# A macaron block in fp32: fc1, q and k of the middle batches as four column tiles of plain fp32 instead of three products of high and low parts

## The chip, the cores and the metric

One Trainium2 chip, one of its cores. The metric is the device time of the kernel in microseconds (us), the median over runs. The engines are named as the profile names them: PE (TensorE, matmuls), PEld (its weight loads), DVE (VectorE), ACT (ScalarE), POOL (GpSimd), SP (SyncE, which only issues DMAs here).

## The reference

The input x is [8, 512, 128]: 8 batches of 512 tokens with 128 features. A transformer block in macaron form is computed, all in fp32:

```
x = x + 0.5 * ffn(layernorm(x))            # the "pre" stage
x = x + attention(layernorm(x))            # x plus its output, normalised, times gamma, plus beta
x = x + 0.5 * ffn(layernorm(x))            # the "post" stage

ffn(x):  h = layernorm(x) * ln_gamma + ln_beta
         y = silu(h @ w1 + b1)             # fc1: 128 -> 512, w1 = (q - 128) * scale of the column
         return x + 0.5 * (y @ w2 + b2)    # fc2: 512 -> 128
attention(x): q, k, v = x @ w_qkv          # 16 heads of 8
         w = relu(q k^T / sqrt(8));  w = w / (sum(w) + 1e-6)
         y = x + (w v) @ w_out + b_out;  return layernorm(y) * gamma + beta
```

## The kernel before

**The grid of steps.** For each batch there are 16 steps: 4 groups of 4 heads times 4 tiles of 128 keys. In a step, `step_scores` (L659) makes the scores of four heads: four matmuls, each on 32 rows of the array (keys and queries as high and low parts in fp32r), 512 queries wide, into four banks of PSUM. ACT takes the relu of two banks (L981), DVE of the other two (L1280), into `probs`. `step_values(b, s - 1)` (L682) multiplies the probs of the step before with the values: four matmuls in plain fp32, each with 32 columns of weights, so that each has a column tile of the array of its own. A plain fp32 matmul stands in the records as two LDWEIGHTS and two MATMULs, so these four are "x8".

**What runs beside it.** All else is cut into small tasks that lists put beside the steps: `PE_ORDER[s]` has the tasks that PE does between the scores and the values of step s ("early") and after them ("late"), and `ACT_ORDER`, `DVE_ORDER` and `POOL_ORDER` say the same for their engines. The orders are written out by hand, each engine does its own strictly in this order, and semaphores tie them together. A name such as `pre.fc1.0@1` is the first quarter of fc1 of the pre stage, for the next batch; `post.fc1.0@-1` is that of the post stage, for the batch before. `*_START` are the lists for batch 0, `*_END` for batch 7, and `*_FIRST` and `*_LAST` stand ahead of and behind the grid: batch 0's pre stage and batch 7's post stage are done there in halves of the tokens (`edge`). "Middle batches" are pre stages of batches 1 to 7 and post stages of batches 0 to 6.

**An ffn in a middle batch.** `hT`: PE turns the normalised rows with four transposes (L596) into the stage's one PSUM bank; ACT copies them as fp32r, `t_hi` (L866); DVE subtracts that from the bank and gets `t_lo` (`low_t`, L1056), which frees the bank. `fc1.f` (f is 0 to 3, 128 of the 512 columns each) is three fp32r matmuls over the whole array, each 512 tokens wide: w_hi t_hi (L608), w_lo t_hi (L609), w_hi t_lo (L631). ACT takes the silu into `y` (L870). `fc2.f` is 16 small plain fp32 matmuls in column tiles (`by_tokens`, L603, x32).

**q and k in a middle batch.** `uT`: four transposes of `u1`; ACT copies twice, to `t_hi` (L878) and in full to `t_u` (L879); POOL subtracts the one from the other for `t_lo` (L1413). `k`, then `q`: the three products again, of which the third (L698) waits for POOL's low part. ACT and then DVE split the result in high and low parts (L887, L1103), and SP sends these to `k_op` and `q_op` by DMA; the scores of step 0 of the next batch wait for them. `v` works on `t_u` in column tiles (L603).

Within a batch the steps of PE that the change touches are: step 0 fc2.0 then pre fc1.0 (both late); step 1 fc2.1 to fc2.3 and pre fc1.1, then the values; step 2 pre fc1.2, then `post.op` (w_out), then the values; step 3 pre fc1.3, then the values; step 11, after the values, uT and post fc1.0; step 12, after the values, k and post fc1.1; step 13, after the values, q and post fc1.2; step 15 post fc1.3 and hT of the next batch, then the values. In batch 0 there is no post stage yet: fc1.0 to fc1.3 stand late in steps 1 to 4. The post fc1 of batch 6 stands in `PE_LAST`, behind the grid.

Of the kernel before, what the change touches and what calls it, by code (L numbers as in the profile page):

```python
# [11 lines left out]
P = 128  # L12
B, S, D = 8, 512, 128
H, HD = 16, 8
F = 512
# [104 lines left out]
    "weights.w1_hi", "first.hT.0", "first.hT.1", "first.fc1.0.1", "first.fc1.1.1",  # L120
    "first.fc1.2.1", "first.fc1.3.1", "first.uT.0", "first.t_u.0", "first.uT.1", "first.k0.0", "first.q0.0",
    "first.t_u.1", "first.q0.1", "first.v.0", "first.k0.1"
# [66 lines left out]
    ["first.k_lo.1"],  # L189
    ["pre.hT@1", "first.q_lo.1"],  # L190
    [],
# [11 lines left out]
    ["a.0"],  # L203
    ["pre.hT@2"],
]
# [10 lines left out]
    [],  # L216
    ["post.hT@-1"],
    [],
    ["oT.0", "den.0", "pre.k_lo@1"],
    ["pre.q_lo@1"],  # L220
    ["a.0"],
    ["pre.hT@2"],
]
# [15 lines left out]
    ["den.0"],  # L239
    ["a.0", "post.hT@-1"],  # L240
]
# [10 lines left out]
POOL_START = [  # L252
    "post.u_bias", "v_in.2", "pre.x_stats@2", "v_in.3", "pre.x1_stats@1", "pre.u_apply@1", "pre.uT@1", "pre.x_apply@2",
    "v_in.0@1", "v_in.1@1", "pre.x1_beta@1", "pre.xr@2"
# [8 lines left out]
    ["pre.u_apply@1"],  # L263
    ["pre.x_stats@2", "pre.uT@1"],
    [],
# [43 lines left out]
def build(nc, x, w_qk, w_v, w_out, fc1_q, fc2_q, fc2_scales, columns, lines, out):  # L309
# [4 lines left out]
    with ExitStack() as ctx:  # L314
        def sb(name, shape, dtype=F32):
            return ctx.enter_context(nc.sbuf_tensor(name, shape, dtype))
# [11 lines left out]
        s2_rows = sb("s2_rows", [P, FT, D])  # L328
        w1_hi, w1_lo = sb("w1_hi", [P, F], F32R), sb("w1_lo", [P, F], F32R)

        wqk = sb("wqk", [P, 4, D])
# [13 lines left out]
        class Stage:  # L345


            def __init__(self, n, fills, buffers):
                self.fills = fills
                self.two_x = [sb(f"{n}_x{i}", [P, TT, D]) for i in range(buffers)]  # L350
                self.h = sb(f"{n}_h", [P, TT, D])
                self.xr = sb(f"{n}_xr", [P, TT, D])
                self.t_hi, self.t_lo = sb(f"{n}_t_hi", [P, S], F32R), sb(f"{n}_t_lo", [P, S], F32R)
                self.y = sb(f"{n}_y", [P, FT, S])
                self.bank = psum(f"{n}_bank", [P, S])
                self.full, self.free = sem(f"{n}_bank_full"), sem(f"{n}_bank_free")
                self.mixed = sem(f"{n}_mixed")
                self.t_hi_in = sem(f"{n}_t_hi_in")
                self.full_a, self.free_a = sem(f"{n}_full_first_half"), sem(f"{n}_free_first_half")
                self.t_hi_a = sem(f"{n}_t_hi_first_half")  # L360
                self.rows, self.rows_by_t, self.res = sem(f"{n}_rows"), sem(f"{n}_rows_by_t"), sem(f"{n}_residual")
# [137 lines left out]
        b1_added, b1_link, b1_ready, b2_ready = sem("b1_added"), sem("b1_link"), sem("b1_ready"), sem("b2_ready")  # L499
        w_link, w2_link, wqk_link = sem("w_link"), sem("w2_link"), sem("wqk_link")  # L500
        w1_ready, w2_ready, wqkv_ready = sem("w1_ready"), sem("w2_ready"), sem("wqkv_ready")
        ident_ready, ident_zero, warm_ready, v_ready = sem("ident_ready"), sem("ident_zero"), sem("warm_ready"), sem("v_ready")
# [76 lines left out]
        def _(pe):  # L579
# [19 lines left out]
            def by_tokens(into, tokens, t, w, start, stop):  # L599
# [4 lines left out]
                return last  # L604

            def two_products(into, w_hi, w_lo, t_hi):

                mm(into, w_hi, t_hi, start=True, stop=False)  # L608
                mm(into, w_lo, t_hi, start=False, stop=False)  # L609

            def ffn(st, b, what):
                if what == "hT":
                    if st is pre and b == 1:

                        pe.wait_ge(*emptied(pre, 0, "v"))
                    else:
                        next_fill(st, b, "hT")
                    if st is post:
                        pe.wait_ge(y_done, b + 1)
                    transposes(st, b, st.h, st.rows)  # L620
                elif what.startswith("fc1"):
                    f = int(what[-1])
                    cols, into = slice(P * f, P * (f + 1)), fc1_bank(st, b, f)
                    if st is post and b == B - 2:

                        pe.wait_ge(probs_done[f // 2][f % 2], STEPS * B)
                        pe.wait_ge(post.free, len(POST_FILLS) * b + post.n("hT"))
                    else:
                        next_fill(st, b, what)
                    two_products(into, w1_hi[:, cols], w1_lo[:, cols], st.t_hi[:, :])  # L630
                    mm(into, w1_hi[:, cols], st.t_lo[:, :], start=False, stop=True).then_inc(st.full, 1)  # L631
                elif what.startswith("fc2"):
                    f = int(what[-1])
                    if f == 0 and not (st is post and b == B - 2):
                        next_fill(st, b, "fc2")
                    pe.wait_ge(st.free, len(st.fills) * b + st.n(f"fc1.{f}"))
                    for t in range(TT):
                        last = by_tokens(st.bank, st.y[:, f, :], t, w2[:, f, :], f == 0 and t == 0, f == FT - 1 and t == TT - 1)
                    if f == FT - 1:
                        last.then_inc(st.full, 1)  # L640
# [45 lines left out]
            def task(stage, what, b):  # L686
                if stage == "pre":
# [4 lines left out]
                    elif what in ("q", "k"):  # L692
                        i = "qk".index(what)
                        next_fill(pre, b, what)
                        pe.wait_ge(u_hi_in, b + 1)
                        two_products(pre.bank[:, :], wqk_hi[:, i, :], wqk_lo[:, i, :], pre.t_hi[:, :])
                        pe.wait_ge(u_lo_in, b + 1)
                        mm(pre.bank[:, :], wqk_hi[:, i, :], pre.t_lo[:, :], start=False, stop=True).then_inc(pre.full, 1)  # L698
                    elif what == "v":
# [21 lines left out]
            def edge(st, b, what, h):  # L721
# [17 lines left out]
                elif what.startswith("fc1"):  # L739
                    f = int(what[-1])  # L740
                    weights, to = slice(P * f, P * (f + 1)), scores[f // 2][:, f % 2, cols]
                    pe.wait_ge(*of_half(st.t_hi_a, st.t_hi_in, h, b))
                    if st is pre:
# [108 lines left out]
        def _(act):  # L852
# [5 lines left out]
            def ffn(st, b, what):  # L858
                per = len(st.fills)
                if what == "hT":  # L860
                    act.wait_ge(st.full, per * b + st.n("hT"))
                    if st is pre and b == 1:

                        act.wait_ge(q_made, 1)

                    activation(st.t_hi[:, :], st.bank[:, :], ACT.Copy).then_inc(st.t_hi_in, 1)  # L866
                elif what.startswith("fc1"):
# [5 lines left out]
            def task(stage, what, b):  # L873
                if stage == "pre":
                    per = len(PRE_FILLS)
                    if what == "uT":
                        act.wait_ge(pre.full, per * b + pre.n("uT"))
                        activation(pre.t_hi[:, :], pre.bank[:, :], ACT.Copy).then_inc(u_hi_in, 1)  # L878
                        activation(t_u[:, :], pre.bank[:, :], ACT.Copy).then_inc(pre.free, 1)  # L879
# [74 lines left out]
            def prepare_w1_hi():  # L954
# [3 lines left out]
                activation(w1_hi[:, :], w1[:, :], ACT.Copy, scale=g_col).then_inc(w_link, 1)  # L958

            def work(b, names):  # L960
                for stage, what, tb in tasks(b, names):
                    if stage == "weights":
                        prepare_w1_hi()
                    elif stage in ("first", "last"):
                        edge(pre if stage == "first" else post, tb, what[:-2], int(what[-1]))
                    else:
                        task(stage, what, tb)
# [19 lines left out]
        def _(dve):  # L987
# [65 lines left out]

            def low_t(st, hi_in, count, done):
                dve.wait_ge(hi_in, count)
                v.tensor_tensor(st.t_lo[:, :], st.bank[:, :], st.t_hi[:, :].bitcast(F32), ALU.subtract  # L1056
                                ).then_inc(done, 1)

            def task(stage, what, b):
# [22 lines left out]
                elif stage == "pre":  # L1082
                    per = len(PRE_FILLS)
                    if what == "x_stats":
                        dve.wait_ge(x_loaded[b % 2], 16 * (b // 2 + 1))
                        row_stats(norm_x, b, pre.x(b))
                    elif what == "hT":
                        low_t(pre, pre.t_hi_in, b + 1, pre.free)
                    elif what == "x1":
# [16 lines left out]
                elif stage == "post":  # L1106
# [18 lines left out]
                    elif what == "x2_stats":  # L1125
                        dve.wait_ge(x2_done, b + 1)
                        row_stats(norm_x2, b, post.x(b))
                    elif what == "hT":
                        low_t(post, post.t_hi_in, b + 1, post.free)
                    elif what == "out":  # L1130
# [34 lines left out]
            def edge(st, b, what, h):  # L1165
# [27 lines left out]
                elif what == "hT":  # L1193
                    dve.wait_ge(*of_half(st.t_hi_a, st.t_hi_in, h, b))
                    v.tensor_tensor(st.t_lo[:, cols], turn_bank(st, h)[:, cols], st.t_hi[:, cols].bitcast(F32), ALU.subtract
# [90 lines left out]
        def _(pool):  # L1286
# [103 lines left out]
            def task(stage, what, b):  # L1390
# [11 lines left out]
                elif stage == "pre":  # L1402
# [6 lines left out]
                    elif what == "xr":  # L1409
                        residual(norm_x, pre, b)  # L1410
                    elif what == "uT":
                        pool.wait_ge(pre.free, len(PRE_FILLS) * b + pre.n("uT"))
                        p.tensor_tensor(pre.t_lo[:, :], t_u[:, :], pre.t_hi[:, :].bitcast(F32), ALU.subtract  # L1413
                                        ).then_inc(u_lo_in, 1)
                    elif what == "x1_stats":
# [100 lines left out]
```

## Time and profile before

| | us |
|---|---|
| median of 3 runs | 370.05 (369.62 to 370.37) |
| span of the profiled execution (first to last instruction) | 369.5 |
| from the values of step 1 of one middle batch (152.05) to those of the next | 43.0 |
| PE busy | 360.0 (97%) |
| DVE busy | 283.8 (77%) |
| ACT busy | 231.4 (63%) |
| POOL busy | 219.8 (59%) |
| granted TensorE clock | 1.000 of full |

"Busy" of PE is the union of its matmuls' spans from start to modelled end. Matmuls are pipelined, and the next one starts before the last one's end; so what a group of matmuls costs is read from its start to the start of the next group, and a short wait between two groups does not show as idle time. The chain that ended last is 87% PE, 4% DVE and 2% each of ACT, DMA, POOL and issue.

### The profile page before, as it was taken

The page shows a single profiled execution, that of the slowest core. Times are in us where ns is not written, and L with a number is a line of the kernel's source. Part 1 is how long each engine was busy: PE and PEld are TensorE (multiplying, and loading weights), DVE is VectorE, ACT ScalarE, POOL GpSimd, SP SyncE. Part 2 cuts the span into 40 slices and gives each one's busy share as a digit, 9 for nine tenths or more (in the row PEclk, how much of TensorE's full clock was granted, in tenths as well). Part 3 has the DMA queues.
Part 4 walks back from the last instruction along what each step waited for, and adds up shares of the span by engine and source line. Part 5 has one row for each costly group of instructions (what it writes and reads, how often), then busy time and mean ns, then how long its engine had stood idle before and what let it go on. Part 6 is the DMA issues. An engine that isn't in the chain of part 4 may idle for free.

```text
span 369.5 us, 11752 instructions
## 1 busy us (share of the span) xinstructions
PE 360.0 (97%) x4518; PEld 185.2 (50%) x4518; DVE 283.8 (77%) x689; ACT 231.4 (63%) x425; POOL 219.8 (59%) x447
## 2 busy tenths in 40 slices
PE   8999998999999999999999999999999999999996
PEld 8854433453564445653564434644456535532476
DVE  5876677897778977699777977689776797578774
ACT  3377465667847586466865678475864668588523
POOL 7595065547973589437992479635894377315541
PEclk9999999999999999999999999999999999999999
DMA  7016005500351005500173003610063001710001
GB/s 211 4 31 173 3 0 128 131 3 2 88 143 60 3 0 136 147 8 1 31 173 87 4 0 67 165 59 2 4 156 104 4 0 32 191 38 2 2 2 61
DMA packets 14103, 22.66 MB, mean 61 GB/s; under 512 B 2528, under 2 KB 3808, under 8 KB 14048
## 3 DMA queue, kind: packets, MB, share of 16 engines
q1 hardware_dynamic: 11456, 17.83, 20.1%
q10 hardware_dynamic: 2592, 4.07, 3.4%
q8 instruction: 37, 0.61, 0.7%
q14 instruction: 18, 0.15, 0.1%
HBM read 3.54 MB, written 2.10 MB: 15 GB/s over the span
## 4 chain that ended last, share of the span: by engine, by line
PE 87%; DVE 4%; ACT 2%; DMA 2%; issue 2%; POOL 2%; SPq 0%; POOLq 0%; DVEq 0%; ACTq 0%
PE o_bank L682 30%; PE scores L659 16%; PE pre_bank L603 9%; PE post_bank L603 9%; PE pre_bank L608 5%; PE pre_bank L609 3%; DMA q_op<-q_parts 2%; PE pre_bank L631 2%; PE post_bank L608 2%; PE pre_bank L596 1%; PE post_bank L609 1%; PE post_bank L631 1%; PE o_bank L590 1%; PE post_bank L596 1%; PE scores L608 1%
## 5 line engine op out<-in xcount | busy, mean ns | idle before, releaser
L1280 DVE TENSOR_SCALAR probs<-scores 128x512 f32<-128x512 f32 x242 | 155.8, 683 | 48.3 <-PE scores L659 45.0
L981 ACT ACTIVATE probs<-scores 128x512 f32<-128x512 f32 x262 | 141.7, 596 | 65.9 <-PE scores L659 65.9
L682 PE MATMUL o_bank<-probs,v_op 128*32 128x512 f32 x1024 | 135.9, 602 | 0.2
L659 PE MATMUL scores<-q_op,k_op 32*128 32x512 f32 x504 | 76.0, 494 | 1.9 <-DMA q_op<-q_parts 0.8
L659 PEld LDWEIGHTS scores<-q_op,k_op 32*128 32x128 f32 x504 | 31.9, 181 | 81.5 <-issue 54.4
L870 ACT ACTIVATE pre_y<-pre_bank,b_sum,col_consts 128x512 f32<-128x512 f32 x28 | 21.9, 782 | 23.6 <-PE pre_bank L631 23.5
L682 PEld LDWEIGHTS o_bank<-probs,v_op 128*32 128x32 f32 x1024 | 21.9, 108 | 28.4 <-issue 24.6
L603 PE MATMUL pre_bank<-w,pre_y 128*32 128x128 f32 x960 | 30.8, 274 | 0.0
L603 PEld LDWEIGHTS pre_bank<-w,pre_y 128*32 128x32 f32 x960 | 25.7, 110 | 8.1 <-issue 7.7
L603 PE MATMUL post_bank<-w,post_y 128*32 128x128 f32 x960 | 29.3, 273 | 0.0
L603 PEld LDWEIGHTS post_bank<-w,post_y 128*32 128x32 f32 x960 | 25.9, 110 | 5.6 <-issue 5.4
L1309 POOL TENSOR_SCALAR norm_x_var<-norm_x_mv 128x4 f32<-128x4 f32 x21 | 4.1, 197 | 39.5 <-DVE norm_x_mv L1051 39.0
L1309 POOL TENSOR_SCALAR norm_y_var<-norm_y_mv 128x4 f32<-128x4 f32 x7 | 1.4, 200 | 43.6 <-DVE norm_y_mv L1051 43.6
L1312 POOL TENSOR_TENSOR norm_x_rs<-norm_x_var,minus_half 128x4 f32<-128x4 f32 x21 | 21.2, 1009 | 1.8
L870 ACT ACTIVATE post_y<-post_bank,b_sum,col_consts 128x512 f32<-128x512 f32 x24 | 18.7, 780 | 0.7
L1447 POOL TENSOR_TENSOR y_rows<-y_rows,rows 128x512 f32<-128x512 f32 x7 | 9.0, 1292 | 16.5 <-ACT y_rows L906 14.3
L1382 POOL TENSOR_TENSOR v_op<-v_rows,v_op 128x128 f32<-128x128 f32 (+1 forms) x33 | 13.6, 420 | 6.4 <-ACT v_rows L892 6.4
L1349 POOL TENSOR_TENSOR norm_x_rs<-norm_x_var,minus_half 128x4 f32<-128x4 f32 x16 | 16.2, 1015 | 1.3
L1365 POOL TENSOR_SCALAR pre_xr<-pre_x,norm_x_mix 128x128 f32<-128x128 f32 x32 | 15.6, 501 | 0.8
L608 PE MATMUL pre_bank<-pre_t_hi,w_hi 128*128 128x512 f32 x28 | 14.0, 499 | 0.9 <-DVE pre_t_lo L1056 0.5
L1340 POOL TENSOR_SCALAR u<-x,norm_x_rs,norm_x_shift 128x128 f32<-128x128 f32 x28 | 12.3, 455 | 1.5 <-POOL norm_x_shift L1316 1.5
L1340 POOL TENSOR_SCALAR post_h<-post_x,norm_x_rs,norm_x_shift 128x128 f32<-128x128 f32 x28 | 12.3, 455 | 1.2 <-POOL norm_x_shift L1316 1.1
(219 smaller groups left out, 555.3 us busy)
## 6 DMA issues: line engine op xcount, KB each, us to landing
k_op<-k_parts SPq DMA_DIRECT2D x62, 128.0 KB, 2.7
q_op<-q_parts SPq DMA_DIRECT2D x62, 128.0 KB, 2.7
out_dram<-o_rows ACTq DMA_DIRECT2D x7, 256.0 KB, 2.0
pre_x<-in_x_dram ACTq DMA_DIRECT2D x6, 256.0 KB, 2.8
w_int<-in_L_ffn_fc_q_dram SPq DMA_DIRECT2D x2, 256.0 KB, 3.9
rows<-in_lines_dram ACTq DMA_DIRECT2D x1, 256.0 KB, 6.0
s_rows<-in_L_ffn_fc_scales_dram SPq DMA_DIRECT2D x1, 256.0 KB, 6.6
wqk<-in_w_qk_dram SPq DMA_DIRECT2D x1, 256.0 KB, 6.7
```

What stands on the lines that cost most here:

```text
L603: last = mm(into[VW * j:VW * (j + 1), P * t:P * (t + 1)], tokens[:, part], w, start=start, stop=stop)
L608: mm(into, w_hi, t_hi, start=True, stop=False)
L609: mm(into, w_lo, t_hi, start=False, stop=False)
L659: mm(score_bank(b, s, i, j), k_op[rows, g, P * kt:P * (kt + 1)], q_op[rows, g, :], start=True, stop=True).then_inc(scores_done[i], 1)
L682: last = mm(o_bank[pair][VW * j:VW * (j + 1), :], v_op[:, kt, heads_of(g).start + 2 * j, :], probs[:, s % 2, j, :], start=(odd == 0 and kt ...
L870: activation(st.y[:, f, :], fc1_bank(st, b, f), ACT.Silu, bias=b1_sum[:, f:f + 1], scale=s1_col[:, f:f + 1]).then_inc(st.free, 1)
L981: activation(probs[:, s % 2, 2 * i + j, :], score_bank(b, s, i, j), ACT.Relu).then_inc(probs_done[i][j], 1)
L1280: v.tensor_scalar(probs[:, s % 2, 2 * i + j, :], score_bank(b, s, i, j), 0.0, None, ALU.max).then_inc(probs_done[i][j], 1)
L1312: p.tensor_tensor(norm.rs[:, i, :], norm.var[:, i, :], minus_half[:, i, :], ALU.pow).then_inc(norm.rs_in, 1)
L1340: last = p.tensor_scalar(dst[:, t, :], rows[:, t, :], norm.rs[:, i, t:t + 1], norm.shift[:, i, t:t + 1], ALU.mult, ALU.add)
L1349: p.tensor_tensor(norm.rs[:, 0, :], norm.var[:, 0, :], minus_half[:, 0, :], ALU.pow).then_inc(norm.half_in, 1)
L1365: last = p.tensor_scalar(st.xr[:, t, :], st.x(b)[:, t, :], norm.mix[:, 0, t:t + 1], norm.mix[:, 1, t:t + 1], ALU.mult, ALU.add)
```

## The change

In middle batches (`ffn` and `task` on PE, not `edge`) the three products are replaced by `by_columns`: four plain fp32 matmuls, each with 32 of the 128 weight columns, each on all 512 tokens, into 32 partitions of the bank. The tokens are one full fp32 copy: `st.t` (new) for fc1, and `t_u`, which is there already, for q and k. The weights are `w1_whole` (new, g times w1 in full, made once by ACT ahead of the grid) and `wqk`.

```diff
+            def by_columns(into, w, tokens):
+                for j in range(HG):
+                    part = slice(VW * j, VW * (j + 1))
+                    last = mm(into[part, :], w[:, part], tokens, start=True, stop=True)
+                return last
...
-                    two_products(into, w1_hi[:, cols], w1_lo[:, cols], st.t_hi[:, :])
-                    mm(into, w1_hi[:, cols], st.t_lo[:, :], start=False, stop=True).then_inc(st.full, 1)
+                    if f == 0 and st is pre and b == 1:
+                        pe.wait_ge(w1_whole_in, 1)
+                    by_columns(into, w1_whole[:, cols], st.t[:, :]).then_inc(st.full, 1)
...
-                        pe.wait_ge(u_hi_in, b + 1)
-                        two_products(pre.bank[:, :], wqk_hi[:, i, :], wqk_lo[:, i, :], pre.t_hi[:, :])
-                        pe.wait_ge(u_lo_in, b + 1)
-                        mm(pre.bank[:, :], wqk_hi[:, i, :], pre.t_lo[:, :], start=False, stop=True).then_inc(pre.full, 1)
+                        by_columns(pre.bank[:, :], wqk[:, i, :], t_u[:, :]).then_inc(pre.full, 1)
...
                     if st is pre and b == 1:
                         act.wait_ge(q_made, 1)
-                    activation(st.t_hi[:, :], st.bank[:, :], ACT.Copy).then_inc(st.t_hi_in, 1)
+                        act.wait_ge(*emptied(pre, 1, "k"))
+                    activation(st.t[:, :], st.bank[:, :], ACT.Copy).then_inc(st.free, 1)
...
-                        activation(pre.t_hi[:, :], pre.bank[:, :], ACT.Copy).then_inc(u_hi_in, 1)
                         activation(t_u[:, :], pre.bank[:, :], ACT.Copy).then_inc(pre.free, 1)
...
+            def prepare_w1_whole():
+                activation(w1_whole[:, :], w1[:, :], ACT.Copy, scale=g_col).then_inc(w1_whole_in, 1)
```

The low parts go with it: `low_t` on DVE (`pre.hT`, `post.hT` out of `DVE_START`, `DVE_ORDER` and `DVE_END`) and the subtraction on POOL (`pre.uT` out of `POOL_START` and `POOL_ORDER`). `weights.w1_whole` comes into `ACT_FIRST`, behind the last silu of the first pre stage. No task changes its place in the lists of PE.

## Rows read from the trace of the kernel before

**Rows 1.** The page's busy times: busy us (share of the span) x instructions.

```profile
PE 360.0 (97%) x4518; PEld 185.2 (50%) x4518; DVE 283.8 (77%) x689; ACT 231.4 (63%) x425; POOL 219.8 (59%) x447
```

**Rows 2.** Timeline of PE, step 5: start us, us, engine line op out<-in xcount.

```profile
161.50 1.06 PE L682 MATMUL o_bank<-probs,v_op 128*32 128x512 f32 x8
162.38 1.06 PE L603 MATMUL pre_bank<-w,pre_y 128*32 128x128 f32 x32
163.37 0.51 PE L659 MATMUL scores<-q_op,k_op 32*128 32x512 f32 x4
```

**Rows 3.** Timeline of PE, steps 11 and 12 of the same batch.

```profile
175.37 0.65 PE L596 MATMUL pre_bank<-ident,u 128*128 128x128 f32 x4
175.78 0.48 PE L608 MATMUL post_bank<-post_t_hi,w_hi 128*128 128x512 f32 x1
...
176.66 0.51 PE L659 MATMUL scores<-q_op,k_op 32*128 32x512 f32 x4
177.10 1.07 PE L682 MATMUL o_bank<-probs,v_op 128*32 128x512 f32 x8
178.09 0.50 PE L608 MATMUL pre_bank<-pre_t_hi,wqk_hi 128*128 128x512 f32 x1
...
178.90 0.39 PE L608 MATMUL post_bank<-post_t_hi,w_hi 128*128 128x512 f32 x1
...
179.69 0.51 PE L659 MATMUL scores<-q_op,k_op 32*128 32x512 f32 x4
```

**Rows 4.** Timeline of PE, step 15 of the same batch.

```profile
185.46 0.50 PE L608 MATMUL post_bank<-post_t_hi,w_hi 128*128 128x512 f32 x1
...
186.26 0.60 PE L596 MATMUL pre_bank<-ident,pre_h 128*128 128x128 f32 x4
186.79 1.07 PE L682 MATMUL o_bank<-probs,v_op 128*32 128x512 f32 x8
```

**Rows 5.** Timeline of PE, steps 1 and 2 of the same batch.

```profile
148.40 2.83 PE L603 MATMUL post_bank<-w,post_y 128*32 128x128 f32 x96
151.16 0.50 PE L608 MATMUL pre_bank<-pre_t_hi,w_hi 128*128 128x512 f32 x1
...
152.05 1.06 PE L682 MATMUL o_bank<-probs,v_op 128*32 128x512 f32 x8
153.05 0.50 PE L659 MATMUL scores<-q_op,k_op 32*128 32x512 f32 x4
...
154.38 1.08 PE L603 MATMUL post_bank<-wo,aT 128*32 128x128 f32 x32
155.28 1.04 PE L682 MATMUL o_bank<-probs,v_op 128*32 128x512 f32 x8
```

**Rows 6.** Busy in two stretches: stretch, us, busy (x) per engine, PEclk, DMA share, GB/s.

```profile
155.28:173.75 18.47, 18.47 (x247) 8.07 (x239) 16.75 (x51) 11.37 (x23) 8.75 (x20) 1.00 0.10 31
163.20:172.25 9.05, 9.05 (x131) 4.10 (x119) 8.72 (x26) 4.52 (x9) 4.65 (x11) 1.00 0.01 2
```

**Rows 7.** Timeline of DVE, steps 10 to 12, with idle time before and its releaser.

```profile
173.81 0.68 DVE L1056 TENSOR_TENSOR post_t_lo<-post_bank,post_t_hi 128x512 fp32r<-128x512 f32 x1
...
177.30 1.29 DVE L1280 TENSOR_SCALAR probs<-scores 128x512 f32<-128x512 f32 x2 [1.61 <-PE scores L659]
```

**Rows 8.** What PE waited for, the whole span: us in total, times, longest.

```profile
PE scores L659 <- DMA q_op<-q_parts: 0.8, 1, 0.8
...
PE pre_bank L608 <- DVE pre_t_lo L1056: 0.5, 1, 0.5
```

**Rows 9.** Timeline of PE, k in step 12 of batch 0.

```profile
51.91 0.50 PE L608 MATMUL pre_bank<-pre_t_hi,wqk_hi 128*128 128x512 f32 x1
...
53.09 0.49 PE L698 MATMUL pre_bank<-pre_t_lo,wqk_hi 128*128 128x512 f32 x1 [0.45 <-POOL pre_t_lo L1413]
```

**Rows 10.** Timeline of PE behind the grid: the bias, then three quarters of fc1, then w_out.

```profile
349.00 0.70 PE L807 MATMUL pre_bank<-u_bias,ident 128*128 128x256 f32 x2
...
351.81 0.65 PE L603 MATMUL pre_bank<-wo,aT 128*32 128x128 f32 x16
```

More of the change, by code:

```diff
@@ L120 @@
     "weights.w1_hi", "first.hT.0", "first.hT.1", "first.fc1.0.1", "first.fc1.1.1",
-    "first.fc1.2.1", "first.fc1.3.1", "first.uT.0", "first.t_u.0", "first.uT.1", "first.k0.0", "first.q0.0",
+    "first.fc1.2.1", "first.fc1.3.1", "weights.w1_whole", "first.uT.0", "first.t_u.0", "first.uT.1", "first.k0.0", "first.q0.0",
     "first.t_u.1", "first.q0.1", "first.v.0", "first.k0.1"
@@ L189 @@
     ["first.k_lo.1"],
-    ["pre.hT@1", "first.q_lo.1"],
+    ["first.q_lo.1"],
     [],
@@ L203 @@
     ["a.0"],
-    ["pre.hT@2"],
+    [],
 ]
@@ L216 @@
     [],
-    ["post.hT@-1"],
+    [],
     [],
@@ L221 @@
     ["a.0"],
-    ["pre.hT@2"],
+    [],
 ]
@@ L239 @@
     ["den.0"],
-    ["a.0", "post.hT@-1"],
+    ["a.0"],
 ]
@@ L252 @@
 POOL_START = [
-    "post.u_bias", "v_in.2", "pre.x_stats@2", "v_in.3", "pre.x1_stats@1", "pre.u_apply@1", "pre.uT@1", "pre.x_apply@2",
+    "post.u_bias", "v_in.2", "pre.x_stats@2", "v_in.3", "pre.x1_stats@1", "pre.u_apply@1", "pre.x_apply@2",
     "v_in.0@1", "v_in.1@1", "pre.x1_beta@1", "pre.xr@2"
@@ L263 @@
     ["pre.u_apply@1"],
-    ["pre.x_stats@2", "pre.uT@1"],
+    ["pre.x_stats@2"],
     [],
@@ L329, in build @@
         w1_hi, w1_lo = sb("w1_hi", [P, F], F32R), sb("w1_lo", [P, F], F32R)
+        w1_whole = sb("w1_whole", [P, F])
         wqk = sb("wqk", [P, 4, D])
@@ L352, in __init__ @@
                 self.xr = sb(f"{n}_xr", [P, TT, D])
+                self.t = sb(f"{n}_t", [P, S])
                 self.t_hi, self.t_lo = sb(f"{n}_t_hi", [P, S], F32R), sb(f"{n}_t_lo", [P, S], F32R)
@@ L500, in build @@
         w_link, w2_link, wqk_link = sem("w_link"), sem("w2_link"), sem("wqk_link")
+        w1_whole_in = sem("w1_whole_in")
         w1_ready, w2_ready, wqkv_ready = sem("w1_ready"), sem("w2_ready"), sem("wqkv_ready")
@@ L741, in edge @@
                     weights, to = slice(P * f, P * (f + 1)), scores[f // 2][:, f % 2, cols]
-                    pe.wait_ge(*of_half(st.t_hi_a, st.t_hi_in, h, b))
+                    pe.wait_ge(st.t_hi_in if h else st.t_hi_a, 1)
                     if st is pre:
@@ L962, in work @@
                     if stage == "weights":
-                        prepare_w1_hi()
+                        (prepare_w1_whole if what == "w1_whole" else prepare_w1_hi)()
                     elif stage in ("first", "last"):
@@ L1052, in row_stats @@
                 last.then_inc(norm.measured, 1)
[L1054 to L1057, printed above, removed]
             def task(stage, what, b):
@@ L1086, in task @@
                         row_stats(norm_x, b, pre.x(b))
-                    elif what == "hT":
-                        low_t(pre, pre.t_hi_in, b + 1, pre.free)
                     elif what == "x1":
@@ L1127, in task @@
                         row_stats(norm_x2, b, post.x(b))
-                    elif what == "hT":
-                        low_t(post, post.t_hi_in, b + 1, post.free)
                     elif what == "out":
@@ L1193, in edge @@
                 elif what == "hT":
-                    dve.wait_ge(*of_half(st.t_hi_a, st.t_hi_in, h, b))
+                    dve.wait_ge(st.t_hi_in if h else st.t_hi_a, 1)
                     v.tensor_tensor(st.t_lo[:, cols], turn_bank(st, h)[:, cols], st.t_hi[:, cols].bitcast(F32), ALU.subtract
@@ L1410, in task @@
                         residual(norm_x, pre, b)
[L1411 to L1414, printed above, removed]
                     elif what == "x1_stats":
```

## The prediction

> **What bounds the kernel now.** I read the page's busy times first: PE 97%, DVE 77%, the others about 60% [rows 1]. That alone would call PE the bound everywhere. Since matmuls are pipelined, I then went through PE's timeline for one middle batch and took each group from its own start to the next group's start ("slot"), since short waits hide in those. A batch repeats every 43.0 us (the table above has it). Its 16 steps fall in two kinds of stretch.
>
> From the values of step 2 (155.28) to the scores of step 11 (173.75) there are 18.47 us, of which DVE is busy 16.75; in the 9.05 us from 163.20 it is busy 8.72, without a gap worth the name [rows 6]. This is a chain from w_out over y, its statistics, POOL's and ACT's normalisation, x2, x1, the statistics and the relus. PE's groups there have slots stretched by waits. In this stretch the only edited group is pre fc1.3.
>
> From step 11 on, and through steps 0, 1 and 2 of the next batch, DVE waits for PE (1.61 us idle before the relu of step 12 [rows 7]) and PE's slots stand back to back. Nine of a batch's ten edited groups are there. So the change is worth what it does to PE's slots in steps 11 to 2, and nearly nothing in steps 3 to 10.
>
> **The slots on both sides.** Two things set a slot: the stream itself, and a switch between kinds of tiling. A group of plain fp32 column tiles of 512 tokens is in the trace already, the values matmul, with the same shapes as the new groups. Followed by another group in column tiles it takes 162.38 - 161.50 = 0.88 us [rows 2]. Followed by matmuls over the whole array it takes 178.09 - 177.10 = 0.99 [rows 3], by scores in row tiles 1.00 [rows 5]. A fc2 group followed by scores takes 0.99 [rows 2]. So a change of tiling costs 0.10 to 0.12, and a new group costs 0.88 inside a run of column groups and 0.98 at its end. Three products cost 0.81 (k) and 0.79 (fc1.1) where they stand behind each other [rows 3], 0.80 with transposes behind them [rows 4], 0.88 before scores [rows 3] and 0.89 before the values [rows 5].
>
> The unknown is whether four tiles that all stream the same 512 tokens go like four that stream different ones. Bounds: 0.86 (a bit under the 0.88, if the shared stream saves reads) and 1.07 (the full length of a values group, nothing overlapped [rows 3]). I take 0.88: the values have the shape, and fc2, whose four tiles do stream one and the same w2, 128 wide, goes through as many columns in the same 0.88 (0.99 with its switch [rows 2]).
>
> **The change part by part.**
> Step 11: before, uT 0.41 and fc1.0 0.88, 1.29 in all [rows 3]. After, the transposes have to switch into column tiles as well: 0.53 with a like group before them [rows 4], plus about 0.06 for the entry, 0.59; then 0.98. +0.28.
> Step 12: before, values 0.99, k 0.81, fc1.1 0.79, 2.59 [rows 3]. After, one run of column tiles: 0.88 + 0.88 + 0.97 = 2.73, or 2.71 as a values group behind another column group takes a trifle less. +0.13. Step 13 (q and fc1.2) has the same pattern: +0.13.
> Step 15: before, fc1.3 0.80 and hT 0.53 [rows 4]. After, 0.98 and 0.59. +0.24.
> Steps 11 to 15 together: +0.78.
> Step 0: fc2.0 no longer switches (-0.11), fc1.0 ends at scores, 0.98 for 0.89: -0.03.
> Step 1: before, three fc2 groups 2.76, fc1.1 0.89, values 1.00, 4.65 [rows 5]. After, 2.65 + 0.88 + 0.97 = 4.50: -0.15.
> Step 2: fc1.2, then w_out, 0.90 [rows 5]: both become 0.88, -0.04. Steps 0 to 2 together: -0.22.
> Step 3: fc1.3, behind it the DVE chain; 0.
>
> Steps 11 to 13 change in batches 1 to 6 (6 x 0.54 = 3.24); step 15 in batches 1 to 5 with a hT behind it (5 x 0.24 = 1.20), in batch 6 without one (-0.04). Steps 0 to 2 change in full in batches 2 to 6 (5 x -0.22 = -1.10); in batch 1 there is no post stage to run with, about -0.13. Middle: +3.17 us.
>
> The removed work. DVE's low part (0.68 [rows 7]) goes twice a batch, 1.4 us of DVE; ACT's second copy and POOL's subtraction go once. I price them at nothing in the middle batches, since they stand where DVE has time: the one in step 10 comes after the relu that PE waits for, the one in step 15 has idle time around it. Bounds: 0 and, if all of DVE's relief reached the chain, -1.4 per batch. I take 0 as DVE idles 1.61 us right behind the first [rows 7].
>
> POOL's tasks behind the removed one (v_in.3, the next x_apply, xr) move about 1.3 us ahead, past nothing that waits. The wait added on ACT (hT of batch 1 behind the DVE's k_lo) queues the copy, then first.q and fc1.0's silu; the old order had the low part behind the same k_lo on DVE, so the bank was not free earlier either. 0, or at most once the 0.68 of such a pass [rows 7]. `w1_whole` on ACT is one pass of 128x512 behind the last silu of the first fc1 and ahead of uT, which must wait for fc2, x1, its statistics and POOL: these hide it, 0; uncovered it would be about as long as DVE's pass, 0.7, once. No DMA is moved, but those of q_op follow q: by the slots above q ends later against step 11, and the run from q to step 0 grows by 0.4, so the DMA has more room, not less.
>
> Start. In batch 0 PE waits 0.5 us for DVE's low part ahead of fc1.0 [rows 8]: gone, and the values before it no longer switch (-0.12), while fc1.0 takes 0.98 for 0.90: -0.53. Then in step 12 the low product of k starts 1.18 us behind the high one, as POOL is late [rows 9]; the group, about 1.55 with some 0.37 for its last slot, becomes 0.98, and starts 0.11 sooner: -0.7. What follows is the chain k, q, DMA, for which the scores of batch 1 wait 0.8 [rows 8]; about -0.6 of it gets through, the rest to the DVE. Three more fc1 of batch 0 at -0.01 each. Start: -1.15.
>
> End. From the bias (349.00) to w_out (351.81) there are 2.81 us with nine products [rows 10]. One is 0.23 (fc1.1's 0.79 less a switch of 0.10, over three [rows 3]); without them 0.71 is left. With three column groups 0.71 + 2.64 = 3.35, or 3.20 if the bias takes less of it: +0.45, all on the chain, since w_out opens the last DVE chain. The post hT of batch 6 is off it.
>
> Sum: +3.17 - 1.15 + 0.45 = +2.5 us. The profiled span is 369.5; after, 372.0. The median of the runs is 370.05, 0.55 above that span, so I forecast 372.5.
>
> A rule against the row. At steady stream a product over the whole array is 0.23 us, three of them 0.70, and four fp32 column tiles are 0.88: the column form is slower as arithmetic, by 0.18, and only the switches that it saves pay that back. The Trainium skill ("FP8 and Floating Point Precision", TensorE Precision Notes) states that true FP32 takes four passes through the array, one for each pairing of high and low halves, where the old code does three of the four. By that rule alone the group would cost 4 x 0.23 = 0.93, and all 70 groups would add 16 us. The trace has 0.88, slightly better than the rule, and its switches take most of the difference away.
>
> **The rivals.**
> A, the likeliest: as above, 372.5. Chance 0.55.
> B, faster: DVE's relief gets through. If the 1.4 us a batch that DVE saves shortened the stretch in which it sets the pace, six batches would give back 8.4: 370.05 + 2.5 - 8.4 = 364.2. For: DVE is busy 16.75 of 18.47 there [rows 6]. Against: the removed work does not lie in that stretch but right behind it (173.81 [rows 7]) and in step 15. A part of it (0.5 a batch) would give 369.5. Chance 0.14.
> C, no change: the entry into the transposes costs nothing (0.53 stays) and column groups take 0.86. That is -0.12 per batch and -0.02 on 60 groups, 2 us less, 370.5. For: the slots are read to 0.01 to 0.03. Chance 0.15.
> D, slower by more: four tiles on one token stream get in each other's way (1.07 per group, the upper bound). On the 58 groups outside the DVE stretch, 0.1 to 0.19 each: 378 to 383. For: no row has one stream of 512 in four tiles. Against: fc2 has one of 128 in four tiles and loses nothing [rows 2]. Chance 0.1.
> E, the rule of four passes without the switches: each group outside the DVE stretch +0.18 to +0.23, 381 to 385. The Trainium skill's page named above speaks for it. Against: steps 12 and 1, where the switches are in the rows. Chance 0.06.
>
> **How the numbers follow.** What a measurement of this kernel tells from no change is about 0.2%, 0.7 us. Case A spreads by some 1.5 us, 371 to 374; its lower edge and C fill the interval around the old time; B lies below. Faster 0.15, same 0.15, slower 0.70. The range 369.6 to 375.5 takes A whole, C, and the partial form of B, and leaves out the full B, most of D, and E.
>
> **What would show it.** In the timeline after, the values, k and fc1.1 of step 12 start 0.88 apart with the scores 0.97 behind; the transposes of steps 11 and 15 take 0.59; steps 3 to 10 keep their 18.5 us; fc1.0 of batch 0 starts without a wait and scores of batch 1 about 1.1 us earlier than before; the batch period goes from 43.0 to 43.55. It would be wrong if a column group with a shared stream takes over 0.95 in a run, if the stretch of steps 3 to 10 gets shorter than 18 us, or if scores of a step 0 wait for the DMA.

## The result

| | before | after |
|---|---|---|
| median, us | 370.21 (369.62 to 370.37, 4 runs) | 372.67 (372.30 to 372.85, 4 runs) |
| ratio to before | 1 | 1.0063, 95% interval 1.0049 to 1.0078 |
| span of the profiled execution | 369.5 | 370.9 |
| PE / DVE / ACT / POOL busy | 360.0 / 283.8 / 231.4 / 219.8 | 363.0 / 275.2 / 229.4 / 208.6 |

The changed kernel is slower by 2.5 us, 0.6%. The median before is 0.16 above the one in the table of the old kernel, since a fourth run has come in. DVE, ACT and POOL all have less to do, PE has more.

The page's busy times after (busy us, share of the span, instructions), against [rows 1]:

```profile
PE 363.0 (98%) x4868; PEld 166.9 (45%) x4868; DVE 275.2 (74%) x675; ACT 229.4 (62%) x419; POOL 208.6 (56%) x440
```

The timeline of PE after, steps 11 and 12 of a middle batch, which answers to [rows 3]. The new groups are line L613.

```profile
174.29 0.66 PE L599 MATMUL pre_bank<-ident,u 128*128 128x128 f32 x4
174.87 1.07 PE L613 MATMUL post_bank<-post_t,w_whole 128*32 128x512 f32 x8
175.87 0.51 PE L670 MATMUL scores<-q_op,k_op 32*128 32x512 f32 x4
176.31 1.06 PE L693 MATMUL o_bank<-probs,v_op 128*32 128x512 f32 x8
177.19 1.04 PE L613 MATMUL pre_bank<-t_u,wqk 128*32 128x512 f32 x8
178.05 1.04 PE L613 MATMUL post_bank<-post_t,w_whole 128*32 128x512 f32 x8
179.02 0.51 PE L670 MATMUL scores<-q_op,k_op 32*128 32x512 f32 x4
```

From start to start: uT 0.58 (0.41 before), fc1.0 1.00 (0.88); in step 12 values 0.88 (0.99), k 0.86 (0.81), fc1.1 0.97 (0.79). The whole of step 12 is 3.15 instead of 3.03.

The same for step 15, against [rows 4]:

```profile
184.91 1.06 PE L613 MATMUL post_bank<-post_t,w_whole 128*32 128x512 f32 x8
185.91 0.66 PE L599 MATMUL pre_bank<-ident,pre_h 128*128 128x128 f32 x4
186.50 1.07 PE L693 MATMUL o_bank<-probs,v_op 128*32 128x512 f32 x8
```

fc1.3 is 1.00 and hT 0.59, where 0.80 and 0.53 stood. And steps 1 and 2, against [rows 5]:

```profile
147.52 2.83 PE L606 MATMUL post_bank<-w,post_y 128*32 128x128 f32 x96
150.17 1.04 PE L613 MATMUL pre_bank<-pre_t,w_whole 128*32 128x512 f32 x8
151.03 1.04 PE L693 MATMUL o_bank<-probs,v_op 128*32 128x512 f32 x8
152.00 0.51 PE L670 MATMUL scores<-q_op,k_op 32*128 32x512 f32 x4
152.43 1.07 PE L613 MATMUL pre_bank<-pre_t,w_whole 128*32 128x512 f32 x8
153.32 1.06 PE L606 MATMUL post_bank<-wo,aT 128*32 128x128 f32 x32
```

Here the neighbours are column groups. From start to start the three fc2 groups, fc1.1 and the values take 2.65, 0.86 and 0.97, for 2.76, 0.89 and 1.00 before: a run of column groups pays one change of tiling, at its end.

The stretch from the values of step 2 to the scores of step 11, against the first of [rows 6] (columns as there):

```profile
154.19:172.67 18.48, 18.48 (x253) 7.85 (x245) 16.78 (x51) 11.44 (x23) 8.76 (x20) 1.00 0.10 30
```

It lasts 18.48 us as before (18.47), with DVE busy 16.78 (16.75). DVE's idle time before the relu of step 12 has grown from 1.61 [rows 7] to 1.91, with the low part gone ahead of it:

```profile
173.31 1.29 DVE L1283 TENSOR_SCALAR probs<-scores 128x512 f32<-128x512 f32 x2 [0.49 <-PE scores L670]
176.51 1.29 DVE L1283 TENSOR_SCALAR probs<-scores 128x512 f32<-128x512 f32 x2 [1.91 <-PE scores L670]
```

### The profile page after: what moved, and what is told of

Its sections match the earlier page's. It is cut to its first block, busy times and chain, and to the rows that moved or that the text cites. A ratio compares the mean times of both kernels' runs of the same rounds, so it can differ in the third digit from the quotient of the medians.

```text
span 370.9 us, 12412 instructions
## 1 busy us (share of the span) xinstructions
PE 363.0 (98%) x4868; PEld 166.9 (45%) x4868; DVE 275.2 (74%) x675; ACT 229.4 (62%) x419; POOL 208.6 (56%) x440
## 4 chain that ended last, share of the span: by engine, by line
PE 88%; DVE 5%; DMA 2%; ACT 2%; issue 1%; SPq 0%; POOL 0%; DVEq 0%; ACTq 0%
PE o_bank L693 31%; PE scores L670 17%; PE pre_bank L613 10%; PE pre_bank L606 9%; PE post_bank L606 8%; PE post_bank L613 6%; PE pre_bank L599 2%; DMA s_rows<-in_L_ffn_fc_scales_dram 2%; PE post_bank L599 1%; DVE probs L1283 1%; PE scores L613 1%; PE scores L618 1%; DVE norm_x_stats L1054 0%; ACT probs L993 0%; ACT y_rows L914 0%
## 5 line engine op out<-in xcount | busy, mean ns | idle before, releaser
L693 PEld LDWEIGHTS o_bank<-probs,v_op 128*32 128x32 f32 x1024 | 23.3, 108 | 31.5 <-issue 30.2
L613 PE MATMUL pre_bank<-pre_t,w_whole 128*32 128x512 f32 x224 | 29.5, 598 | 0.5 <-ACT pre_y L879 0.5
L613 PE MATMUL post_bank<-post_t,w_whole 128*32 128x512 f32 x192 | 25.3, 598 | 0.0
L613 PE MATMUL pre_bank<-t_u,wqk 128*32 128x512 f32 x112 | 14.6, 594 | 0.1
```

The source lines that it names most:

```text
L613: last = mm(into[part, :], w[:, part], tokens, start=True, stop=True)
L693: last = mm(o_bank[pair][VW * j:VW * (j + 1), :], v_op[:, kt, heads_of(g).start + 2 * j, :], probs[:, s % 2, j, :], start=(odd == 0 and kt ...
```

## The experiments

All are compared with the kernel before on the same chip; intervals are 95%. "Column tiles" are `by_columns`, as in the change.

**The kernel before once more.** No edit.

> The kernel of before itself, timed against itself, to see how far two identical programs fall apart and how much of a run's time lies outside its span. Ratio 1.000, within 0.2%. The profiled execution of before has a span of 369.5 and the changed kernel's 370.9, which is 1.4 apart, while their medians are 2.5 apart. Theory 1: the time around the span differs between the two profiled executions by chance, and before's is about 0.7 to 1 here again or anywhere up to 2. Theory 2: the changed kernel has more around its span than before has in all its runs.

Measured: 369.90, ratio 0.9998 (0.9987 to 1.0008), span 367.9 for an execution of 369.75. So the time around the span is 1.85, about as for the changed kernel (372.85 and 370.9, 1.95), and the first trace, with 369.5, was a long execution of the old kernel: over 27 executions of before in this comparison the spans go from 367.6 to 369.1. Of the 1.6 us that it had more, 0.7 lie ahead of the grid (the first scores of batch 0 start at 21.47, for 20.77 in the second trace), 0.7 where batch 1 begins, and 0.2 where batch 5 begins. In the first trace PE waits 0.8 for the DMA of q_op where batch 1 begins [rows 8]; in the second, PE's timeline shows no idle time before these scores (L659):

```profile
59.32 1.07 PE L682 MATMUL o_bank<-probs,v_op 128*32 128x512 f32 x8
60.46 0.50 PE L659 MATMUL scores<-q_op,k_op 32*128 32x512 f32 x4
```

The slot of these values is 1.14, though, for 1.00 elsewhere, and 0.99 at this place in the changed kernel: a wait of some 0.15 hides in it, so the DMA wait was smaller in this execution and not wholly absent. Of the two theories the first holds, if with 1.85 and not the 0.7 to 1 thought likelier: the two medians, not the two first spans, tell the change. The comparisons of places below use this second trace.

**Only pre fc1 in column tiles.** The edit in short, not in the kernel's words:

```diff
-    by_columns(into, w1_whole[:, cols], st.t[:, :])            # all middle fc1, q, k
+    by_columns(...) if st is pre else three products           # q, k: three products
```

> Only fc1 of the pre stage (steps 0 to 3, where its neighbours are column tiles) is in column tiles; post fc1, q and k stay three products. Theory of the switches: steps 0 to 2 give back 0.22 in five batches and 0.13 in batch 1, batch 0 gives 0.7 (no wait for DVE's low part), -1.9 in all: 368.3. Rival, a column group costs 0.18 more than three products wherever it stands (0.88 against 0.70): 28 groups, +5.0: 375.2. Rival, the gain of the whole change at the start is all from k and q: 369.0.

Measured: 367.70, ratio 0.9935 (0.9921 to 0.9950). The first 16 steps take 38.83 us (39.69 before), a middle batch 42.76 (43.00). The theory of the switches gave 368.3, which is within the interval; the price by the group (375.2) and the gain all from k and q (369.0) are not. This half of the change is a gain.

**Only post fc1, q and k in column tiles.** The complement of the last one.

> The other half alone: post fc1, q and k in column tiles (steps 11 to 15 and behind the grid), pre fc1 stays three products. Theory of the switches: +0.54 in steps 11 to 13 of six batches, +0.24 in step 15 of five, +0.45 at the end, -1.4 in batch 0 for k and q, +3.5 in all: 373.7. With only-pre-fc1 it should add up to the whole change. Rival, 0.18 a group wherever it stands: 42 groups, +7.6, less 1.4: 376.4.

Measured: 374.94, ratio 1.0130 (1.0113 to 1.0148), 1.2 above the 373.7 expected. Batches 3 to 5 take 43.79 to 43.81, 0.80 more than before, which is the working of the prediction (0.78). The excess lies elsewhere: batch 0 gives 0.76 back and not 1.4, since most of the DMA wait of the first trace is not there in the second; batch 6 takes 0.2 and batch 7 takes 0.28 more than expected (both below); and batch 2 takes 44.15, as a relu on DVE starts some 0.36 late in its step 8 (at 124.83, 1.00 behind the scores), for which the trace names no releaser but these scores. The rival's 376.4 is outside the interval. The two halves add up: -2.5 and +4.7 make +2.2 where the whole change has +2.5.

**DVE's low parts put back, unused.** The edit in short:

```diff
-    activation(st.t[:, :], st.bank[:, :], ACT.Copy).then_inc(st.free, 1)
+    activation(st.t[:, :], st.bank[:, :], ACT.Copy).then_inc(st.t_hi_in, 1)
+    # DVE, at its old places:
+    v.tensor_tensor(st.t_lo, st.bank, st.t, ALU.subtract).then_inc(st.free, 1)
```

> The changed kernel with DVE's two subtractions per batch put back where they were (they free the bank again, and nobody reads what they write). Theory: worth nothing in the middle batches, about 0.5 to 0.6 in batch 0 where fc1.0 waits for DVE: 372.7 + 0.6 = 373.3. Rival, DVE's relief is part of what keeps the change at only +0.7%: DVE is over 90% busy in steps 3 to 10, 0.5 to 1.4 per batch come back: 376 to 381.

Measured: 372.99, ratio 1.0078 (1.0063 to 1.0094), not to be told from the 1.0063 (1.0049 to 1.0078) without them. A middle batch takes 43.55 to 43.57, as without them (43.53 to 43.56). Only batch 0 has them: 38.94 for 38.25, and PE's timeline shows the wait of [rows 8] back again ahead of fc1.0:

```profile
25.94 1.07 PE L632 MATMUL pre_bank<-pre_t,w_whole 128*32 128x512 f32 x8 [0.49 <-DVE pre_t_lo L1103]
```

So 9.6 us of DVE work (14 passes of 0.69) are worth nothing but this one wait, and the rival's 376 to 381 is out.

**ACT's second copy and POOL's subtraction put back, and k waits for it.** The edit in short:

```diff
+    activation(pre.t_hi[:, :], pre.bank[:, :], ACT.Copy).then_inc(u_hi_in, 1)    # ACT, uT
+    p.tensor_tensor(pre.t_lo, t_u, pre.t_hi, ALU.subtract).then_inc(u_lo_in, 1)  # POOL
+    pe.wait_ge(u_lo_in, b + 1)                                                   # PE, before k and q
```

> The changed kernel with ACT's second copy of uT and POOL's subtraction put back, and k waiting for the subtraction although it doesn't read it. Theory: in batch 0 k is late again as before, +0.6 to 0.8; in the middle batches the subtraction ends about 3.1 us after uT starts, and k, which now follows the values 0.11 sooner and has no high products to do first, would wait some 0.2 to 0.3 in each of six batches: 372.7 + 2.2 = 374.9. Rival, the wait is as free in the middle batches as it was before the change: 373.4.

Measured: 376.91, ratio 1.0180 (1.0164 to 1.0195), 2 us above what I expected. Batches 2 to 5 take 43.96 to 44.01, 0.44 more than the changed kernel and not 0.2 to 0.3. The timeline of a middle batch in steps 11 and 12 has the reason:

```profile
176.34 0.66 PE L618 MATMUL pre_bank<-ident,u 128*128 128x128 f32 x4
...
178.19 1.28 POOL L1466 TENSOR_TENSOR pre_t_lo<-t_u,pre_t_hi 128x512 fp32r<-128x512 f32 x1 [0.42 <-ACT t_u L925]
...
179.62 1.07 PE L632 MATMUL pre_bank<-t_u,wqk 128*32 128x512 f32 x8 [0.20 <-POOL pre_t_lo L1466]
```

The subtraction ends 3.13 after uT's start, as I had reckoned (3.1). But k starts 0.15 behind that end, 3.28 after uT, where the changed kernel has it at 2.90 (177.19 - 174.29): 0.38 later. PE's idle time before k, 0.20, shows only half of this, since it counts from the modelled end of the values; step 12 as a whole goes from 3.15 to 3.56. Batch 0 takes 1.38 more, for 0.6 to 0.8 expected. What PE waited for in the whole execution has a second item that I had not thought of:

```profile
PE pre_bank L632 <- POOL pre_t_lo L1466: 2.4, 7, 1.2
...
PE scores L695 <- DMA q_op<-q_parts: 1.1, 1, 1.1
```

The 2.4 are 1.2 in batch 0 and 0.2 in each of six batches. The 1.1 stand once, before batch 7. Of q's two transfers there one took 2.6 us to land and the other 4.5, for 2.5 and 2.6 in the changed kernel. The slow one was issued at 317.7 and so was in at 322.2, and the scores start at 322.25; with 2.6 it would have been in at 320.3, before they were due (321.2). So it was the slow landing and not the later q alone; why it was slow is not shown. The rival, a wait free in the middle batches, is out: the three products had hidden POOL behind their two high products; a single group that needs all of t at its start has nothing to hide it with. That the change takes t_u whole is thus not a side issue.

**Two tasks exchanged in the changed kernel.**

```diff
-    ([], ["pre.uT@1", "post.fc1.0@-1"]),       # PE_ORDER, step 11
+    ([], ["post.fc1.0@-1", "pre.uT@1"]),
-    (["post.fc1.3@-1", "pre.hT@2"], []),       # PE_ORDER, step 15
+    (["post.fc1.3@-1"], ["pre.hT@2"]),
-    ["pre.hT@2", "post.fc1.3@-1"],             # ACT_ORDER, step 15
+    ["post.fc1.3@-1", "pre.hT@2"],
```

> The changed kernel with two tasks of PE exchanged so that a change of tiling falls away: in step 11 post fc1.0 goes ahead of uT, directly behind the values; in step 15 the values go ahead of hT (and ACT takes fc1.3's silu first). No instruction is added or removed. Theory, a change of tiling costs 0.10 to 0.14: -0.13 in six batches and -0.14 in five: 372.7 - 1.5 = 371.2. Rival, the column groups are dear by themselves and the order doesn't matter: 372.7. Other rival, uT or hT is late for k or for fc1.0 then: over 373.

Measured: 371.21, ratio 1.0028 (1.0019 to 1.0037). With the same instructions in another order 1.5 us are gone by the medians and 1.3 by the trace, from the first scores to w_out behind the grid. In steps 11 and 15 each of the 11 places is shorter by 0.12 to 0.16, as worked out from one change of tiling less; batch 6 gives 0.12 of it back in step 13 (below). Both rivals, 372.7 and over 373, are out. PE's timeline of the new step 11:

```profile
172.45 1.06 PE L718 MATMUL o_bank<-probs,v_op 128*32 128x512 f32 x8
173.33 1.04 PE L632 MATMUL post_bank<-post_t,w_whole 128*32 128x512 f32 x8
174.30 0.66 PE L618 MATMUL pre_bank<-ident,u 128*128 128x128 f32 x4
174.89 0.51 PE L695 MATMUL scores<-q_op,k_op 32*128 32x512 f32 x4
```

0.88, 0.97, 0.59: 2.44 us where the changed kernel has 1.00, 0.58, 1.00, 2.58. A middle batch takes 43.28 instead of 43.55.

One rival to the word "tiling" remains. The column groups are also the plain fp32 ones, so where such a group ends both the tiling and the form of the products change. The kernel before has a place where only the tiling changes, from fp32r over the whole array to fp32r in row tiles, in PE's timeline of step 0:

```profile
147.41 0.40 PE L609 MATMUL pre_bank<-pre_t_hi,w_lo 128*128 128x512 f32 x1
147.64 0.39 PE L631 MATMUL pre_bank<-pre_t_lo,w_hi 128*128 128x512 f32 x1
147.96 0.51 PE L659 MATMUL scores<-q_op,k_op 32*128 32x512 f32 x4
```

The third product takes 0.32 to the next start, the second 0.23. So a change of tiling alone costs 0.09 there. That it makes up all of the 0.10 to 0.14 behind a column group was not tried.

**Column tiles only where they pay.** pre fc1 of all batches, and q and k of batch 1.

```diff
+def fc1_by_columns(stage, b):
+    return stage == "pre"
+def qk_by_columns(b):
+    return b == 1
```

> Column tiles where their neighbours are column tiles or where the low part was late: pre fc1 in all batches, q and k of batch 1 (done during batch 0); post fc1 and the other q and k stay three products. Theory: only-pre-fc1 measured 367.7; q and k of batch 1 give back another 0.6, as the first 16 steps took 38.25 with them and 38.83 without: 367.1, 0.8% under the kernel before. Rival, the two gains of batch 0 overlap: 367.7.

Measured: 367.01, ratio 0.9918 (0.9903 to 0.9932), 3 us under the kernel before and, by the two ratios, 5.4 under the changed one. The first 16 steps take 38.24, as in the changed kernel, a middle batch 42.75. These first steps speak against the rival, by which the two gains overlap (367.7); the median alone hardly would, as its interval ends at 367.5. PE's timeline has k of batch 1 directly behind the values, and the scores (L695) 0.98 later, where [rows 9] have a wait of 0.45 inside k:

```profile
49.53 1.06 PE L718 MATMUL o_bank<-probs,v_op 128*32 128x512 f32 x8
50.41 1.04 PE L632 MATMUL pre_bank<-t_u,wqk 128*32 128x512 f32 x8
51.39 0.51 PE L695 MATMUL scores<-q_op,k_op 32*128 32x512 f32 x4
```

## Why the prediction was right, step by step

Forecast 372.5, measured 372.67. The terms, from the starts of the scores of step 0 of each batch in PE's timeline (second trace of before against the changed kernel):

| | predicted | measured |
|---|---|---|
| batch 0 | -1.15 | 39.69 to 38.25: -1.44 |
| batch 1 | +0.65 | 39.88 to 40.72: +0.84 |
| batches 2 to 5 | +0.56 each | 43.00 to 43.02, then 43.53 to 43.56: +2.17 in all |
| batch 6 | +0.28 | 42.57 to 43.04: +0.47 |
| batch 7 up to its last scores | 0 | 29.33 to 29.61: +0.28 |
| from there to w_out | +0.45 | 5.88 to 6.29: +0.41 |

These sum to +2.73. What is left of the two spans is +0.6 ahead of the grid and -0.4 in the last store. The first is larger or smaller from one execution to the next: the first scores start at 20.77 and 21.47 in the two traces of the old kernel, at 20.72 to 21.40 in the others. The second is not: from the start of DVE's last addition to the end of the span the old kernel takes 2.84 and 2.93, all seven kernels with an edit 2.55 to 2.63. So some 0.3 us are gained there that nobody had priced, and with them the sum comes to +2.4, as the medians have it (+2.46). The cause was not looked for.

*Luck in the total.* The forecast lies within 0.2 us of the measured time, which is closer than its terms are. Batch 0 gave 0.3 more than predicted and the last store another 0.3, while batches 1 and 6 took 0.2 each and batch 7 0.3 more. The forecast span of 372.0 was 1.1 above the measured one (370.9), since it was worked out from the span of a long execution; the 0.55 that was then added for the time around the span was as much too small (1.95 measured), and the two errors cancel. And two figures of the rivals do not fit: the partial form of B, 369.5, lies just outside the range that was said to take it in, and 58 groups at 0.18 to 0.23 give 380.5 to 383.4 for E and not 381 to 385.

*The slots.* Right in each place: 0.85 to 0.89 inside a run of column groups, 0.97 to 1.00 at its end, 0.58 to 0.59 for the transposes that now enter from column tiles. That four tiles with one stream of 512 tokens go like four with different ones was the unknown, and is now in the rows after. Rival D (the shared stream) is out by these rows, and so is the entry without a cost of rival C (0.59 for 0.53), though its 0.86 for a group between column groups came true; that the order of tasks alone moves 1.5 us shows that the switch has a price of its own beside the group's. Rival E, a group dearer by 0.18 wherever it stands, is out by the first half alone, faster by 0.65% with 28 such groups. The Trainium skill's rule of four passes ("FP8 and Floating Point Precision", TensorE Precision Notes) comes near the stream itself: 4 x 0.23 = 0.92 as an estimate by that rule, 0.86 to 0.88 in the rows. For the change of tiling the Trainium skill has a rule too ("TensorEngine Tiling (Array Packing)", Key Properties), by which changing the tiling mode drains the engine. The rows agree that it costs time: 0.10 to 0.14 at the end of a column group, 0.06 for the transposes' entry from one; that it is a drain they do not show.

*DVE's relief worth nothing* (against rival B): the stretch kept its 18.48 us, and the dead passes lengthened only batch 0.

*Batch 0.* Right in kind, a little small. The wait for DVE's low part is gone: step 1 goes from 3.77 to 3.18. For k and q I had counted that -0.6 of the gain would come through a DMA wait of 0.8; most of that wait belonged to the one execution that had been traced. Without it the batch still gains, as k ends sooner on PE itself: step 12 goes from 3.03 to 2.29, and step 15, with the small wait left, from 2.58 to 2.42. So the -0.6 was the right size for another reason; against the trace that the prediction read, batch 0 is 2.1 shorter, as the two gains add up.

*Batch 1.* Of the 0.19 above the prediction 0.14 lies in step 8 (1.97 to 2.11), which was not followed up.

*Batch 6.* POOL's tasks moving ahead was priced at 0, "past nothing that waits". It met DVE instead. The timeline after in step 12 of batch 6:

```profile
308.83 1.29 POOL L1378 TENSOR_TENSOR post_xr<-post_xr,b_quarter 128x512 f32<-128x512 f32 x1
...
309.09 1.07 DVE L1075 TENSOR_SCALAR den<-o_t 128x32 f32<-128x32 f32 x1
...
310.46 0.63 DVE L1108 SCALAR_TENSOR_TENSOR k_parts<-pre_bank,k_parts 128x512 fp32r<-128x512 f32 x1
```

A DVE instruction whose median is 0.19 lasts until POOL's addition ends (310.12 and 310.16); k_parts and with them q come later, and step 13 is 3.35 where other batches have 3.15. The same instruction takes 1.05, 1.04 and 1.20 in the other three kernels without POOL's subtraction (the second half, the dead low parts, the exchanged tasks), and step 13 takes 3.33, 3.31 and 3.47. The exchanged tasks have the common end again, 308.45 and 308.50:

```profile
307.17 1.28 POOL L1426 TENSOR_TENSOR post_xr<-post_xr,b_quarter 128x512 f32<-128x512 f32 x1
...
307.30 1.20 DVE L1117 TENSOR_SCALAR den<-o_t 128x32 f32<-128x32 f32 x1
```

The kernel with POOL's subtraction put back is the test from the other side. There the addition starts 3 us after the DVE instruction has ended, this one takes 0.19, and step 13 is 3.14:

```profile
312.39 0.19 DVE L1118 TENSOR_SCALAR den<-o_t 128x32 f32<-128x32 f32 x1
...
315.64 1.28 POOL L1427 TENSOR_TENSOR post_xr<-post_xr,b_quarter 128x512 f32<-128x512 f32 x1
```

That run also has ACT's second copy and a later k, so POOL's addition was not moved alone; but it is long where the two overlap, four times, and short where they do not. The step of the prediction that was wrong is thus "past nothing that waits": it costs 0.2 us, once.

*Batch 7.* Open. Steps 11 and 12 take 0.28 more, in the four kernels that have neither ACT's second copy nor POOL's subtraction in the middle batches (the changed one, the second half, the dead low parts, the exchanged tasks), and not in the others. Which of the two it hangs on is not shown, as the run that put them back put back both. ACT's relu of step 11 starts 0.56 after ACT's last instruction and 0.89 after the scores, for 0.27 and 0.59 in the old kernel, and the trace names no releaser but these scores. The first line is the changed kernel's, the second that of the second trace of before:

```profile
340.87 1.08 ACT L993 ACTIVATE probs<-scores 128x512 f32<-128x512 f32 x2 [0.56 <-PE scores L670]
337.91 1.08 ACT L981 ACTIVATE probs<-scores 128x512 f32<-128x512 f32 x2 [0.27 <-PE scores L659]
```

## What to carry to other kernels

Where matmul groups of different tilings follow each other, price a group from its start to the next one's start, and each change of tiling with it: here one column group put between scores and transposes made its step 0.25 us longer (step 15), a pair behind the values 0.12 longer (step 12), and one between other column groups made its step 0.17 shorter (step 1), so that the same edit is worth -2.5 us in one half of the places and +4.7 in the other. Work taken from an engine with idle time behind it was worth only the one place where somebody waited for it; look for that place (often the first batch, where the pipeline is not full), and apply the edit there alone. One trace is one execution: a wait that it has only once may not be in the next.

## What the runs showed of the hardware

A DVE instruction of 128x32 on SBUF that began during a POOL addition of 128x512 took 1.04 to 1.20 us instead of 0.19 in four kernels, and ended within 0.05 of it in the two traces shown above. Four column tiles that stream the same 512 tokens take 0.86 to 0.88 us per group in a run, as four that stream different ones (0.88). A change of tiling behind a group of plain fp32 column tiles costs 0.10 to 0.14 us.
